# Two sequences' expert passes: full tiles first, the first sequence's remainders joined to the second's tiles

## The chip, the cores and the metric

One core of a Trainium2 chip. The metric is the device time of one execution in microseconds (us). TensorE (PE, with PEld for its weight loads), VectorE (DVE), ScalarE (ACT), GpSimd (POOL) and SyncE (SP, which issues most DMAs) each run their own program and wait for one another through semaphores.

## The reference

Input x is 2 sequences of 2048 tokens of 256 values. The kernel computes two blocks:

```
x = x + layernorm(attention(layernorm(x)))          # one head of 128, rope, full softmax
x = x + layernorm(ffn(layernorm(x)))

ffn(z): twice:
    zn     = rmsnorm(z) * norm_w
    scores = softmax(zn @ router_w)                  # 8 experts
    two best experts of each token, gates normalised to sum 1
    z      = z + sum over the two: gate * (silu(zn @ w1[e]) * (zn @ w3[e])) @ w2[e]   # 256 -> 512 -> 256
```

## The kernel before

**Shape of the program.** The first 385 us hold the attention of both sequences. In the attention of the second, DVE slips in the routing of the first sequence, and splits the expert weights into pairs of fp16 numbers. Then come four expert passes in the order (loop 0, sequence 0), (0, 1), (1, 0), (1, 1), numbered k = 0 to 3, and a tail in which the second sequence's last results are combined, normalised and stored.

**Tiles.** A pass treats one sequence: 2 x 2048 = 4096 rows (a token once for each of its experts), sorted by expert and padded to whole tiles of 128 rows for each expert. With 8 experts that is at most 32 + 7 = 39 tiles (`TILES`), and the pass always runs 39, whatever the data: a tile that holds no rows costs as much as a full one. A tile t goes like this:

- POOL `fetch` (L1620) gathers 128 rows of fp16 pairs (`x_pair`), four tiles ahead; SP `turn` (L1566) turns them with a transposing DMA into `e_xT`, two tiles ahead.
- PE `inner` (L1966): 12 matmuls into `psum_a`, 12 into `psum_b`. ACT takes silu of the first (L1708); DVE `gate` (L1888) multiplies the two.
- At the start of the next tile PE `turn_h` (L1974) turns the product; ACT (L1703) and DVE `h_lo` (L1881) split it into two fp16 halves. PE then does `inner` of the next tile and only after that `outer` (L1985, 12 matmuls) of this one. ACT copies the result out (`y_copy`, L1714), POOL `send` (L1629) scatters it to `expert_rows`.

So every engine's program is a list of tiles, and PE's order is turn_h(t-1), inner(t), helpers, outer(t-1), helpers.

**Helpers beside the tiles.** While pass k runs, the other sequence's next routing (number r = k + 1) is made in the tiles of the pass, in an order written by hand in `expert_pass`: `quad` in tiles 3 to 14 (SP loads results in `load_half`, L1547; DVE `combine` adds them, L1754 and L1760; PE `turn_z`, L1928, and `logits`, L603; ACT squares and copies), then `stage` with one step per tile in tiles 15 to 32: logits, softmax, `pick_best` twice (L440 to L449), gate values (L455 to L462), counts (L471, L477), `expert_starts` (L483 to L488), `expert_rows_of_tiles` (L493 to L495), `rows_of_tokens` (L501 to L511), `experts_of_tiles` (L559 to L562), `mark_tiles` (L516), four times `mark_lanes` of 8 (L523), and indices (L540 to L551). Beside steps 3 to 10 run `row_hi` (ACT, L1680), `row_lo` (DVE, L1815) and `store_rows` (SP, L1555 on), which write the rows that the next pass will gather. On DVE a helper comes after `gate` of its tile and before the `h_lo` that follows:

```python
for u in range(UNROLL):
    ...
        h_lo(s - 1)
    gate(s)
    if join:
        join(u, "end")
```

`link(...)` makes DVE wait for the end of the instruction just issued, so linked instructions run strictly one after another. A small part of the four passes is a hardware loop (`Fori`) over groups of three tiles: on ACT and DVE the quads, on PE only the quads and the `last` groups of k = 3 and one group in each other pass. In the tail SP loads each quarter of the last results, DVE combines it and takes its statistics.

Of the kernel before, what the change touches and what calls it, by code (L numbers as in the profile page):

```python
# [34 lines left out]
TILES = 2 * S // P + NE - 1  # L35
ROWS = TILES * P
# [15 lines left out]
ARENA = 17760  # L52
# [16 lines left out]
def sandwich_kernel(nc, x, wq, wk, wv, wo, norm_w, router_w, w1, w3, w2, rope, out, sorted_rows, expert_rows, token_rows):  # L69
    with ExitStack() as ctx:  # L70
# [58 lines left out]
        sources = sb("token_of_row", [P, B, TILES], U32)  # L129
        targets = sb("result_row_of_row", [P, B, TILES], U32)  # L130
        expert_sb = sb("expert_of", [P, B * TILES], I32)
        gates = gates_sb[:, :].rearrange("p (h k t) -> p h k t", h=B, k=2)
        expert_of = expert_sb[:, :].rearrange("p (h t) -> p h t", h=B)
        rank_sb = sb("rank_down", [P, NE])
        tile_row_sb = sb("tile_row", [P, TILES])
# [17 lines left out]
        def routing_space(large, both, small, row):  # L153

            wide = [large(C) for _ in range(8)]
            return Routing(*wide, both(2 * C), small(4 * NT).rearrange("p (k t) -> p k t", k=4),
                           small(2 * NT).rearrange("p (k t) -> p k t", k=2), small(2 * NT).rearrange("p (k t) -> p k t", k=2),
                           [small(2 * NT).bitcast(I32) for _ in range(3)], small(4 * NE).rearrange("p (k e) -> p k e", k=4),
                           small(NE).bitcast(I32), small(TILES * NE), small(TILES), row(4 * TILES))

        front = take(NT * TILES + NT)
        hot_t = front[:, 0 : NT * TILES].bitcast(F16)
        squares, sum_sq = front[:, 0:D], front[:, NT * TILES : NT * TILES + NT]
        zT = take(2 * 2 * D).rearrange("p (half u c t) -> p half u c t", half=2, u=2, c=DC)
        later_routing = routing_space(take, take, take, lambda n: front[:, D : D + n])
# [40 lines left out]
        first_routing = routing_space(pieces(shared), pieces(xT_words[0][:, D : 2 * D]), pieces(wqkv_words),  # L206
                                      pieces(tab[:, NT * P + NT * TILES :]))
# [131 lines left out]
        x_split = [t.bitcast(F16).rearrange("r d -> (r d)")[0 : S * 2 * D].rearrange("(r d) -> r d", d=2 * D) for t in sorted_rows]  # L339
# [67 lines left out]

        def shifted_logits(dve, link, r):
# [4 lines left out]
            if r:  # L413
                dve.wait_ge(s_rms, r + 1)
                nc.vector.tensor_scalar(factor[:, h, :], root, X_SCALE, None, ALU.mult).then_inc(s_factor, 1)
# [64 lines left out]
        def expert_starts(dve, link, r):  # L480
            R = routing[r > 0]
            total, padded, upper, start = (R.start_f[:, q, :] for q in range(4))
            link(nc.vector.tensor_copy(total, tok_exp(R.sum)[:, NT - 1, :]))  # L483
            link(nc.vector.tensor_scalar(R.start_i, total, float(P - 1), None, ALU.add))
            link(nc.vector.tensor_scalar(R.start_i, R.start_i, -P, None, ALU.bitwise_and))
            link(nc.vector.tensor_copy(padded, R.start_i))
            link(nc.vector.tensor_tensor_scan(upper, padded, zero_tile[:, 0:NE], 0.0, ALU.add, ALU.add))
            link(nc.vector.tensor_tensor(start, upper, padded, ALU.subtract))  # L488

        def expert_rows_of_tiles(dve, link, r):  # L490
            R = routing[r > 0]

            link(nc.vector.tensor_tensor(R.sum, R.sum, R.both[:, C : 2 * C], ALU.subtract))  # L493
            link(nc.vector.tensor_tensor(R.sum, R.sum, R.both[:, 0:C], ALU.add))
            link(nc.vector.tensor_tensor(tok_exp(R.sum), tok_exp(R.sum), per_expert(R.start_f[:, 3, :]), ALU.add))  # L495
# [1543 lines left out]
```

## Time and profile before

| | |
|---|---|
| median of 3 runs | 1161.94 us (1158.58 to 1163.95) |
| the profiled execution | 1165.51 us, its span 1163.8 us |
| mean granted TensorE clock over the span | 0.961 |
| PE busy, DVE busy, ACT busy, POOL busy | 91%, 61%, 49%, 46% |
| expert passes | first matmul at 392.17 us, the last tile's send at 1118.95 us |

A busy share is a mean over stages that have different limits. What sets the time of a stage is read from the chain that ended last and from the spacing of one instruction from tile to tile.

### The profile page before, as it was taken

How to read it: one execution, taken by the hardware profiler on the slowest of the kernel's cores; microseconds unless marked ns; L12 is line 12 of the kernel's file. 1: busy time of each engine (PE TensorE's matmuls, PEld its weight loads, DVE VectorE, ACT ScalarE, POOL GpSimd, SP SyncE). 2: the span in 40 equal slices, each digit the busy share in tenths (PEclk: the TensorE clock that was granted, in tenths of full speed). 3: DMA queues.
4: the chain of work that ended last, by engine and by line, in shares of the span. 5: the costliest groups of instructions: out<-in, count | busy, mean ns of one | idle time of the engine just before them, and what ended most of it. 6: DMA issues, size and time to landing. Idle time of an engine off the chain costs nothing.

```text
span 1163.8 us, 24709 instructions
## 1 busy us (share of the span) xinstructions
PE 1057.8 (91%) x7506; PEld 723.6 (62%) x7507; DVE 705.4 (61%) x1598; ACT 574.5 (49%) x1117; POOL 532.8 (46%) x699
## 2 busy tenths in 40 slices
PE   4799998788999599999999999999999999999930
PEld 3478886556888266666667666666766666656620
DVE  5779988869887244576344476444467436544436
ACT  3566666557987234553345553345464333333312
POOL 2412234956776453444443544444444444544315
PEclk9899999879999799999999999999999999999975
DMA  9900000000000222353365254365355346433344
GB/s 313 338 1 0 0 0 1 1 15 20 17 18 6 55 84 76 96 154 88 92 154 150 79 145 109 91 161 136 88 131 125 88 127 173 107 94 88 82 148 159
DMA packets 146311, 110.81 MB, mean 95 GB/s; under 512 B 92592, under 2 KB 132144, under 8 KB 146224
## 3 DMA queue, kind: packets, MB, share of 16 engines
q1 hardware_dynamic: 131248, 68.72, 22.9%
q0 software_dynamic: 14976, 40.91, 11.8%
q8 instruction: 56, 0.92, 0.3%
q14 instruction: 31, 0.25, 0.1%
HBM read 56.11 MB, written 33.03 MB: 77 GB/s over the span
## 4 chain that ended last, share of the span: by engine, by line
PE 62%; DVE 2%; DMA 1%; issue 1%; ACT 0%; POOL 0%; ACTq 0%; SPq 0%; DVEq 0%; POOLq 0%
PE psum_s L1966 36%; PE psum_o L1985 18%; PE psum_s L1974 6%; PE psum_t L603 2%; PE psum_t L1928 1%; DVE arena L1754 1%; DMA arena<-expert_rows 0%; DVE f_stats L1780 0%; DMA arena<-arena 0%; DMA arena<-sorted_rows,token_of_row 0%; DVE arena L1760 0%; DMA expert_rows<-arena,result_row_of_row 0%; PE psum_t L531 0%; DVE f_tmp L360 0%; DVE arena L1888 0%
## 5 line engine op out<-in xcount | busy, mean ns | idle before, releaser
L1966 PE MATMUL psum_s<-w_all,arena 128*128 x1872 | 432.9, 381 | 12.8 <-DMA arena<-arena 11.2
L1629 POOL DMA_INDIRECT expert_rows<-arena,result_row_of_row x156 | 156.1, 1000 | 359.0 <-ACT arena L1714 356.1
L1966 PEld LDWEIGHTS psum_s<-w_all,arena 128*128 128x128 f16 x1872 | 174.3, 98 | 213.2 <-issue 22.8
L1888 DVE SCALAR_TENSOR_TENSOR arena<-psum_s,gate_scale,arena 128x512 f32<-128x512 f32 x156 | 117.1, 751 | 206.6 <-ACT arena L1708 98.8
L1985 PE MATMUL psum_o<-w_all,arena 128*128 x1872 | 229.9, 273 | 1.5 <-DVE arena L1881 1.5
L1985 PEld LDWEIGHTS psum_o<-w_all,arena 128*128 128x128 f16 x1872 | 181.9, 98 | 47.7 <-issue 3.6
L1881 DVE TENSOR_TENSOR arena<-psum_s,arena 128x512 f16<-128x512 f32 x156 | 107.5, 689 | 147.8 <-ACT arena L1703 114.8
L1714 ACT ACTIVATE arena<-psum_o 128x256 f32<-128x256 f32 x156 | 59.8, 383 | 251.1 <-PE psum_o L1985 247.3
L1620 POOL DMA_INDIRECT arena<-sorted_rows,token_of_row x156 | 153.2, 982 | 52.3 <-issue 46.0
L1708 ACT ACTIVATE arena<-psum_s,silu_scale 128x512 f32<-128x512 f32 x156 | 107.4, 688 | 125.9 <-PE psum_s L1966 73.2
L1703 ACT ACTIVATE arena<-psum_s 128x512 f16<-128x512 f32 x156 | 93.1, 597 | 21.4 <-PE psum_s L1974 14.9
L1340 PE MATMUL psum_s<-arena 128*128 128x512 f16 x384 | 94.4, 398 | 1.4 <-DVE arena L1116 1.4
L1974 PE MATMUL psum_s<-ident,arena 128*128 128x128 f32 x624 | 94.2, 274 | 1.0 <-DVE arena L1888 0.8
L823 ACT ACTIVATE arena<-psum_t 128x512 f32<-128x512 f32 (+1 forms) x128 | 69.7, 595 | 45.6 <-PE psum_t L1335 45.2
L875 ACT ACTIVATE arena<-psum_s,arena,alpha 128x1024 f32<-128x1024 f32 x64 | 76.5, 1199 | 25.4 <-DVE arena L1144 25.3
L1127 DVE TENSOR_REDUCE arena<-psum_s 128x1 f32<-128x1024 f32 x64 | 77.8, 1216 | 12.7 <-PE psum_s L1340 12.6
L1335 PE MATMUL psum_t<-ident,arena 128*128 128x128 f32 x512 | 68.2, 276 | 9.1 <-ACT arena L875 5.8
L1974 PEld LDWEIGHTS psum_s<-ident,arena 128*128 128x128 f32 x624 | 73.3, 142 | 4.1 <-DVE arena L1888 2.4
L1335 PEld LDWEIGHTS psum_t<-ident,arena 128*128 128x128 f32 x512 | 59.3, 143 | 17.9 <-ACT arena L875 7.2
L1340 PEld LDWEIGHTS psum_s<-arena 128*128 (+1 forms) x384 | 39.2, 103 | 44.2 <-issue 7.6
L1380 PE MATMUL psum_o<-arena 128*128 128x128 f32 x512 | 64.1, 278 | 0.0
L1380 PEld LDWEIGHTS psum_o<-arena 128*128 128x128 f32 x512 | 59.7, 192 | 0.0
(238 smaller groups left out, 1223.4 us busy)
## 6 DMA issues: line engine op xcount, KB each, us to landing
w_all<-in_L_ffn_w SPq DMA_DIRECT2D x24, 512.0 KB, 10.1
arena<-expert_rows SPq DMA_DIRECT2D x48, 256.0 KB
sorted_rows<-w_all SPq DMA_DIRECT2D x24, 256.0 KB
arena<-expert_rows SPq DMA_DIRECT2D x8, 512.0 KB, 5.5
out<-x_sb SPq DMA_DIRECT2D x8, 512.0 KB, 6.4
arena<-sorted_rows,token_of_row POOLq DMA_INDIRECT x156
arena<-arena SPq DMA_TRANSPOSE x156
expert_rows<-arena,result_row_of_row POOLq DMA_INDIRECT x156
```

Of the source, the lines that this page charges most:

```text
L1335: last = nc.tensor.transpose(psum_t[g % 2][:, k * P : (k + 1) * P], probs[:, kc * P : (kc + 1) * P], ident[:, :])
L1340: last = nc.tensor.matmul(psum_s[:, kb * 512 : (kb + 1) * 512], qkT[:, lq, 0, bass.ds(i * P, P)], qkT[:, lk, 1, kb * 512 : (kb + 1) * 512] ...
L1380: last = nc.tensor.matmul(psum_o[:, 0:P], v_whole[:, kc, :], pT_whole[:, (kc - HALVED) * P : (kc - HALVED + 1) * P], start=False, stop=(kc ...
L1620: nc.gpsimd.indirect_dma_start(x_pair[:, u, :, :].rearrange("p l d -> p (l d)"), None, x_split[h], bass.IndirectOffsetOnAxis(ap=sources[:, ...
L1629: nc.gpsimd.indirect_dma_start(expert_rows[h][:, :], bass.IndirectOffsetOnAxis(ap=targets[:, h, t : t + 1], axis=0), y_row[:, u, :], None) ...
L1703: nc.scalar.activation(hT[:, 0, :, :].rearrange("p c t -> p (c t)"), psum_h, ACT.Copy).then_inc(s_h_hi, 1)
L1708: nc.scalar.activation(silu_a, psum_a, ACT.Silu, scale=silu_scale[:, 0:1]).then_inc(s_silu, 1)
L1881: nc.vector.tensor_tensor(hT[:, 1, :, :].rearrange("p c t -> p (c t)"), psum_h, hT[:, 0, :, :].rearrange("p c t -> p (c t)"), ALU.subtract ...
L1888: nc.vector.scalar_tensor_tensor(h_row, psum_b, gate_scale[:, 0:1], silu_a, ALU.mult, ALU.mult).then_inc(s_h, 1)
L1966: last = nc.tensor.matmul(bank, e_xT[:, u, lx * DC + c, :], w_split[:, bass.ds(e * EW + at, FF)], start=(q == 0), stop=(q == 3 * DC - 1))
L1974: last = nc.tensor.transpose(psum_h[:, c * P : (c + 1) * P], h_row[:, c * P : (c + 1) * P], ident[:, :])
L1985: last = nc.tensor.matmul(psum_e, hT[:, lh, c, :], w_split[:, bass.ds(e * EW + at, D)], start=(q == 0), stop=(q == 3 * FC - 1))
```

## The change

The first sequence's pass of a loop (k = 0 and 2) now takes only full tiles of its experts, exactly 25 (`FULL`; 32 tiles' worth of rows over 8 experts always hold at least 25 full ones). The rows that are left are carried: they join the rows of the second sequence, in a pass of 46 tiles (`MIXED`, k = 1 and 3). The carried rows come first there, in at most 14 tiles (`CARRY`), whose free rows the second sequence fills. A loop then has 71 tiles and the kernel 142, where it had 156. Both sequences' gathered rows of a loop lie in one DRAM buffer, and all results in `token_rows`. The first sequence's results are complete after tile 13 of the mixed pass, so its combine starts there in tile 18, not in the next pass. The index arithmetic (`expert_starts`, `expert_rows_of_tiles`, `experts_of_tiles`, `row_indices`) gets more steps. All loops of the passes are written out (no `Fori`), and a table of plans says in which tile each helper runs. The first half of the output is stored from within the last pass, and the tail's four loads are issued together.

```diff
+FULL = TILES - 2 * (NE - 1)                       # 25
+CARRY = TILES - FULL                              # 14
+MIXED = 2 * B * S // P + NE - 1 - FULL            # 46
...
-            link(nc.vector.tensor_scalar(R.start_i, total, float(P - 1), None, ALU.add))
-            link(nc.vector.tensor_scalar(R.start_i, R.start_i, -P, None, ALU.bitwise_and))
-            link(nc.vector.tensor_copy(padded, R.start_i))
-            link(nc.vector.tensor_tensor_scan(upper, padded, zero_tile[:, 0:NE], 0.0, ALU.add, ALU.add))
-            link(nc.vector.tensor_tensor(start, upper, padded, ALU.subtract))
+        def full_tiles_first(dve, link, r):        # r = 0 and 2: 15 linked instructions, 2 others (was 6)
+            nc.vector.tensor_copy(total, counted)
+            link(nc.vector.tensor_copy(R.start_i, counted))
+            link(nc.vector.tensor_scalar(R.start_i, R.start_i, -P, None, ALU.bitwise_and))
+            link(nc.vector.tensor_copy(full, R.start_i))
+            link(nc.vector.tensor_tensor_scan(own, full, zero_tile[:, 0:NE], 0.0, ALU.add, ALU.add))
...
+        def rest_tiles_first(dve, link, r):        # r = 1 and 3: 10 linked, 2 others
+            nc.vector.tensor_tensor(own, rest_rows, rest, ALU.subtract)
+            nc.vector.tensor_tensor(shift, rest_start, rest, ALU.add)
+            link(nc.vector.tensor_tensor(total, tok_exp(R.sum)[:, NT - 1, :], rest, ALU.add))
...
+            link(nc.vector.tensor_tensor(beyond, tok_exp(R.sum), own, ALU.is_ge))
+            nc.vector.tensor_tensor(tok_exp(R.both[:, 0:C]), tok_exp(R.sum), shift, ALU.add)
+            link(nc.vector.tensor_tensor(beyond, beyond, step, ALU.mult))
+            link(nc.vector.tensor_tensor(R.sum, R.both[:, 0:C], R.both[:, C : 2 * C], ALU.add))
...
+                for q, threshold in enumerate((carried[:, 2, :], start)):      # r = 1 and 3
+                    link(nc.vector.tensor_tensor(cmp, tile_row.unsqueeze(2).to_broadcast(shape),
+                                                 threshold.unsqueeze(1).to_broadcast(shape), ALU.is_ge))
+                    link(nc.vector.tensor_reduce(R.expert[:, q, :], cmp, AX.X, ALU.add))
...
+        PASS = (FULL, MIXED, FULL, MIXED)
+        Plan = namedtuple("Plan", "load combine root logits softmax pick1 pick2 gates counts starts ranks places experts marks lanes split index")
+        plans = (Plan(None, 3, None, 12, 13, 13, 14, 14, 15, 15, 16, 16, 17, 17, (0,) * 18 + (11, 11, 10), 3, 21),
+                 Plan(16, 18, 26, 27, 28, 29, 30, 31, 32, 33, 34, 35, 36, 36, (0,) * 37 + (8, 8, 8, 8), 27, 41),
+                 Plan(1, 3, 11, 12, 13, 13, 14, 14, 15, 15, 16, 16, 17, 17, (0,) * 18 + (11, 11, 10), 12, 21),
+                 Plan(16, 18, 26, *(None,) * 14))
+        OUT = 29
...
+                    if k and t == plan.load:
+                        for u in range(UNROLL):
+                            sp.wait_ge(s_sent[u], landed(u, FIRST[k] + (CARRY if k % B else 0)))
+                        for p in range(2):
+                            load_half(k, p)
+                    if k and 2 <= t - plan.combine + 1 < PAIRS:
+                        load_half(k, t - plan.combine + 1)
+                    if k < END and 0 <= t - plan.split - 1 < PAIRS:
+                        store_rows(k, t - plan.split - 1)
+                    if k == END and 2 <= t - OUT < 2 + PAIRS and (t - OUT) % 2 == 0:
+                        store_out((t - OUT - 2) // 2)
```

In the plans a number is a tile of the pass. `combine` = c means one pair of token tiles in each of the tiles c to c + 7 on DVE, with `turn_z`, `logits` and ACT's part one tile later; `split` = s means `row_hi`, `row_lo` and `store_rows` in the tiles s + 1 to s + 8; `lanes` gives the number of lane marks in each tile. Before, `combine`, `turn_z` and `logits` took two of every three tiles.

## Rows read from the trace of the kernel before

**Rows 1.** The page: chain that ended last, by line.

```profile
PE psum_s L1966 36%; PE psum_o L1985 18%; PE psum_s L1974 6%; PE psum_t L603 2%; PE psum_t L1928 1%; DVE arena L1754 1%; DMA arena<-expert_rows 0%; DVE f_stats L1780 0%; DMA arena<-arena 0%; DMA arena<-sorted_rows,token_of_row 0%; DVE arena L1760 0%; DMA expert_rows<-arena,result_row_of_row 0%; PE psum_t L531 0%; DVE f_tmp L360 0%; DVE arena L1888 0%
```

**Rows 2.** That chain in order of time: start, us, what; the start, and two plain tiles.

```profile
385.67 3.04 DMA arena<-sorted_rows,token_of_row
388.73 3.32 DMA arena<-arena
392.17 5.23 PE psum_s L1966 x12
...
1106.53 2.62 PE psum_s L1966 x12
...
1110.89 2.64 PE psum_s L1966 x12
```

**Rows 3.** Timeline of POOL: first send of passes 0, 1, 3, and the last.

```profile
403.78 1.01 POOL L1629 DMA_INDIRECT expert_rows<-arena,result_row_of_row  x1 [8.03 <-ACT arena L1714]
...
585.79 0.97 POOL L1629 DMA_INDIRECT expert_rows<-arena,result_row_of_row  x1 [2.11 <-ACT arena L1714]
...
949.96 0.98 POOL L1629 DMA_INDIRECT expert_rows<-arena,result_row_of_row  x1 [2.10 <-ACT arena L1714]
...
1118.95 0.97 POOL L1629 DMA_INDIRECT expert_rows<-arena,result_row_of_row  x1 [2.45 <-ACT arena L1714]
```

**Rows 4.** Timeline of DVE in pass 1: start, us, line, operation, idle before.

```profile
672.97 0.75 DVE L1888 SCALAR_TENSOR_TENSOR arena<-psum_s,gate_scale,arena 128x512 f32<-128x512 f32 x1 [1.47 <-PE psum_s L1966]
673.63 0.28 DVE L440 TENSOR_REDUCE arena<-arena 128x16 f32<-128x128 f32 x1
...
675.62 0.88 DVE L1815 SCALAR_TENSOR_TENSOR w_all<-arena,row_factor,w_all 128x256 f16<-128x256 f32 x2
676.41 0.68 DVE L1881 TENSOR_TENSOR arena<-psum_s,arena 128x512 f16<-128x512 f32 x1
677.32 0.75 DVE L1888 SCALAR_TENSOR_TENSOR arena<-psum_s,gate_scale,arena 128x512 f32<-128x512 f32 x1 [0.22 <-issue]
...
682.46 0.17 DVE L455 TENSOR_TENSOR arena<-arena 128x16 f32<-128x16 f32 x1
...
683.86 0.88 DVE L1815 SCALAR_TENSOR_TENSOR w_all<-arena,row_factor,w_all 128x256 f16<-128x256 f32 x2
...
687.24 0.41 DVE L471 COPY arena<-psum_y 128x256 f32<-128x256 f32 x1
...
688.52 0.88 DVE L1815 SCALAR_TENSOR_TENSOR w_all<-arena,row_factor,w_all 128x256 f16<-128x256 f32 x2
...
691.62 0.16 DVE L483 COPY arena<-arena 128x8 f32<-128x8 f32 x1
...
692.85 0.93 DVE L1815 SCALAR_TENSOR_TENSOR w_all<-arena,row_factor,w_all 128x256 f16<-128x256 f32 x2
...
700.34 0.48 DVE L501 TENSOR_TENSOR arena<-arena 128x128 f32<-128x128 f32 x2
...
702.07 0.88 DVE L1815 SCALAR_TENSOR_TENSOR w_all<-arena,row_factor,w_all 128x256 f16<-128x256 f32 x2
...
709.06 1.45 DVE L516 TENSOR_TENSOR arena<-tile_of_row,tile_numbers 128x1248 f16<-128x1248 f32 x1
...
713.41 1.87 DVE L523 TENSOR_SCALAR arena<-lane_numbers,lane_of_row,token_numbers 128x128 f16<-128x128 f16 x8
```

**Rows 5.** Windows: us, busy of PE, PEld, DVE, ACT, POOL, granted clock, DMA share, GB/s.

```profile
392.00:396.00 4.00, 3.83 (x10) 1.35 (x11) 0.00 (x0) 0.69 (x1) 2.84 (x3) 0.50 0.38 100
...
280.00:290.00 10.00, 7.97 (x68) 5.91 (x66) 9.58 (x24) 7.08 (x13) 6.76 (x12) 1.00 0.04 14
...
950.00:1001.00 51.00, 50.66 (x317) 30.86 (x316) 31.58 (x65) 19.12 (x35) 23.98 (x24) 1.00 0.64 166
1064.00:1112.00 48.00, 47.92 (x306) 29.78 (x305) 20.88 (x38) 17.66 (x33) 17.97 (x19) 1.00 0.30 75
```

**Rows 6.** The page's DMA issues: KB each, median us to landing.

```profile
arena<-expert_rows SPq DMA_DIRECT2D x8, 512.0 KB, 5.5
```

More of the change, by code:

```diff
@@ L151, in sandwich_kernel, with routing_space @@
         C = NT * NE
-        def routing_space(large, both, small, row):
+        def routing_space(large, both, small, row, tiles, cmp):
             wide = [large(C) for _ in range(8)]
@@ L1604, in _ @@
+            for c in range(QUADS, B * QUADS):
+                store_out(c)
             sp.wait_ge(s_out, 16 * B * QUADS)
@@ L1733, in _, with h_hi @@
-            for k in range(len(order)):
-                experts(k)
+                        square(r, 2 * p + g)
+                    copy_zT(act, r, p, p % 2)
+                if t == plan.logits + 1:
+                    exps(act, r)
+                if 0 <= t - plan.split - 1 < PAIRS:
+                    row_hi(k, t - plan.split - 1)
+            def h_hi(s):
+                act.wait_ge(s_th, s + 1)
+                nc.scalar.activation(hT[:, 0, :, :].rearrange("p c t -> p (c t)"), psum_h, ACT.Copy).then_inc(s_h_hi, 1)
@@ new lines, in beside @@
+                        first_z(1, t - plan.combine)
+                if k and t == plan.root:
+                    mean_square(r)
+                if t == plan.split:
+                    row_factor(dve, r)
+                if t == plan.logits:
+                    shifted_logits(dve, link, r)
+                if t == plan.softmax:
+                    softmax(dve, link, r)
+                if t == plan.pick1:
+                    pick_best(dve, link, r, 0)
+                if t == plan.pick2:
+                    pick_best(dve, link, r, 1)
@@ new lines, in beside @@
+                if t == plan.gates:
+                    gate_values(dve, link, r)
+                if t == plan.counts:
+                    counted_tiles(dve, link, r)
+                if t == plan.starts:
+                    expert_starts(dve, link, r)
+                if t == plan.ranks:
+                    expert_rows_of_tiles(dve, link, r)
+                if t == plan.places:
+                    rows_of_tokens(dve, link, r)
+                if t == plan.experts:
+                    experts_of_tiles(dve, link, r)
@@ new lines, in beside @@
+                if t == plan.marks:
+                    dve.wait_ge(s_rows, r + 1)
+                    dve.wait_ge(s_eid, r + 1)
+                    dve.sem_inc(s_held, 1)
+                    mark_tiles(hot_t, slots_of(r))
+                if t < len(plan.lanes):
+                    mark_lanes(hot_p, sum(plan.lanes[0:t]), plan.lanes[t])
+                if t == plan.index:
+                    read_tokens(dve, link, r)
+                    row_indices(dve, link, r)
+                if 0 <= t - plan.split - 1 < PAIRS:
+                    row_lo(k, t - plan.split - 1)
@@ L2013, in _, with beside @@
-            for k in range(len(order)):
-                experts(k)
+            def beside(k, plan, t):
+                r = B + k - 1
+                if 0 <= t - plan.combine - 1 < PAIRS:
+                    turn_z(r, t - plan.combine - 1)
+                if t == plan.counts:
+                    counts(pe, r)
+                for part in range(PARTS):
+                    if t == min(plan.index - PARTS + 1 + part + (k % B == 0), plan.index):
+                        tokens_of_rows(pe, r, hot_t, hot_p, token_sums[1], part)
```

688 lines of the change are left out of this document (319 added, 369 removed).

## The prediction, made before the changed kernel ran

> **What bounds the kernel now.** I read the page's chain first. Two thirds of it is PE in the expert passes [rows 1], next to nothing else: for 727 us the end moves only with the matmuls. The chain in order of time then gives the cost of one tile without helpers: `inner` starts at 1106.53 and, one tile on, at 1110.89, so 4.36 us, of which 2.62 are `inner` itself [rows 2]. The timeline of POOL gives the passes: from the first send of pass 0 to that of pass 1 are 182.0 us [rows 3], of which 39 x 4.36 = 170.0 are tiles and 12.0 the PE helpers (`turn_z`, `logits`, counts, tokens) and small waits. Pass 3 has no PE helpers; its 38 intervals take 169.0 [rows 3] against 165.7, so 3.3 are lost.
>
> The timeline of DVE shows how near it comes to mattering. A helper starts 0.66 after its `gate`, and the next `h_lo` follows it. With 2.78 us of helpers (673.63 to 676.41) the next `gate` came at 677.32, 4.35 after the last, and waited only 0.22 [rows 4]. So a tile has room for about 2.78 us of helpers; what is beyond delays `h_lo`, behind which PE's `outer` and DVE's own next `gate` are queued, and so every following tile by the excess.
>
> **What is removed.** 156 - 142 = 14 tiles. Helpers stay, once for each routing, so what goes are tiles at the plain price: 14 x 4.36 = 61.0 us. ACT's, DVE's, POOL's and SP's share of these tiles goes too, and all lies behind PE. Bounds: nothing in the pass runs faster than the plain tile, and the mean tile costs 182.0/39 = 4.67, which would be 65.3; I take 61.0, since the helper work is not removed.
>
> **Loops written out.** Pass 3 is the one in which most of PE's groups loop. I take it that its 3.3 us are the price of the looping and come back, and about 0.2 from the other passes' single looped group: 3.5. Bounds: 0, if they are small waits of another kind that stay, and 4.
>
> **DVE helpers, packed closer.** Passes 0 and 2 have 25 tiles where 39 held the same routing, so steps share tiles. Costs from [rows 4]: `pick_best` 1.99 (673.63 to 675.62, 6 linked steps, 0.33 each), so softmax (3 steps) about 0.95; gate values 1.40; counts 1.28; six small linked steps 1.23, so 0.205 each; `rows_of_tokens` 1.73; a compare or reduce goes by its elements, 0.28 for 128 and 1.45 for 1248 (`mark_tiles`), so 0.53 for 368; eight lanes 1.87 to the end of the last, 0.22 apart; `row_lo` 0.80 (675.62 to 676.41).
>
> Pass 0, excess over 2.78:
> tile 13, softmax and first pick 2.94: 0.16. Tile 14, second pick and gates 3.39: 0.61. Tile 15, counts 1.28 and `rest_tiles_first` (10 linked, 2 others) 2.25: 0.75. Tile 16, ranks (5 linked steps of 0.33 and one of 0.2) 1.86 and places 1.73: 0.81. Tile 17, four compares and reduces over 368 elements at 0.57, two small steps 0.4, marks over 46 tiles for 39 (1.71), 4.39: 1.61. Tiles 18 to 21 (lanes 2.45, indices, six linked small steps and five others, about 2) fit. Sum 3.9.
>
> Pass 2 has `row_lo` in tiles 13 to 20 as well, 0.80 more in each: 0.96, 1.41, 1.55, 1.61, 2.41, then 0.47 twice (11 lanes, 3.25) and 0.24: 9.1.
>
> Pass 1 has room: only tile 33, `full_tiles_first` (15 linked, 2 others, 3.28) with `row_lo`, 4.08, exceeds: 1.3.
>
> Together 14.3 us. Bounds: nothing, if PE helpers in the same tiles or ACT's slack give DVE more room than the row shows; and 20, if each such tile also loses some 0.4 to ACT or SP lateness.
>
> **DVE in the second attention.** Routing 0 has 9 more linked steps and one or two others (2.0), two more linked steps and one other for the ranks (0.86), and a compare and a reduce over 200 elements in place of 312 (0.23 less): 2.6. Where it runs DVE is busy 9.58 of 10 us and PE only 7.97 [rows 5], so DVE sets the pace there and I take all 2.6; the bounds are 0, if PE's work there covers it, and 2.6.
>
> **What is moved and costs nothing.** First-sequence combine now sits in tiles 18 to 25 of the mixed passes, in every tile and not in two of three. It is four instructions of the size of `row_lo`'s two, so 4 x 0.40 = 1.6 on DVE (2.4 in pass 3 with two statistics), under 2.78. PE's `turn_z` and `logits` are the same count. The first fetch of a pass waits on POOL for the indices: made in tile 21 of 25, fetch and turn took 3.04 and 3.32 at the start [rows 2], and the rows are needed three tiles (13 us) on; the `send` queued behind the waiting fetch has as long, since `y_row` has three buffers. If that cover goes, each of three pass starts costs up to these 6.4 us. The tail keeps its DVE chain; its first-half stores were off the chain already.
>
> **Sum.** On the profiled execution's 1165.5: minus 61.0, minus 3.5, plus 14.3, plus 2.6 = 1117.9. That execution lies 3.6 above the median of 1161.9, so 1114.3: 1114 us.
>
> **Rivals.**
> *DVE's room is larger.* No stall beyond noise, and attention hides its part: 1114.3 - 14.3 - 2.6 = 1097; with a few remaining, 1099. For it: DVE is busy only 61% of the span. Against: the one row at 2.78 had no more than 0.22 left.
>
> *Loads come late.* A load of results is now issued one tile before its combine, it was two. In pass 3: the load waits for the pair two before (gate + 2.3) and is wanted at the gate two tiles on + 0.66, 9.4, leaving 7.1 us. A load of 512 KB, in pairs of 1 MB, landed in 5.5 [rows 6], and ours are pairs of 256 KB. But DMA share in the loading stretch of pass 3 was 0.64 for 51 us and 0.30 in plain tiles [rows 5]: eight loads took 17.3, 2.2 each, so a tile with its own load wants 1.3 + 2.2 of 4.36, 0.80. If queueing makes each late by 1 to 2 us in one mixed pass (8 tiles), DVE waits in `combine`, `h_lo` behind it: plus 8 to 16, 1122 to 1130.
> The Trainium skill (DMA: Bandwidth & Descriptors, the fixed and variable cost) would give, as an estimate, 2.0 us and 0.5 MB at 436 GB/s, 3.2 us, for such a pair alone, well in time, and the sum would stay as it is; no row here shows one alone.
>
> *Slower than before: the clock falls.* PE now meets idle gaps in passes 0 and 2 up to 2.4 us in a row of tiles. The first `inner` of pass 0, after PE had waited for fetch and turn, took 5.23, twice its 2.62 [rows 2], at a granted clock of 0.50, the 1.2 GHz level [rows 5]. At that level a tile costs 4.4 more, so from 13 such tiles on the 47.6 us of the forecast and another 5.8 are gone, and the time is 1168 or more. Against: from 280 to 290 PE idled 2 of 10 us and the clock stayed at 1.00 [rows 5].
> The skill (TensorE: Matmul & The Clock Gate, Part 1) has the clock fall when the engine idles; the first tile's 0.50 agrees.
>
> **How the numbers follow.** Forecast (14 tiles gone, DVE stalls of about this size) 0.60, own range 1106 to 1121. Room larger, near 1099: 0.16. Loads or a pass start late, near 1125: 0.19. Clock 0.02. Something that eats the gain entirely, near no change: 0.03 with chances split. The range 1100 to 1128 leaves out the lower half of the second case, some of the third, and the last two. A measurement here can tell about 0.5%, 5.8 us; the first three cases are all faster by more: faster 0.95, same 0.02, slower 0.03.
>
> **What would show it.** Sends 4.36 apart in plain tiles, 142 of them; in pass 2 gates 5 to 7 us apart in tiles 14 to 18, with PE waiting for L1881's successor there; pass 3 without the spread of intervals up to 4.8; no wait of `combine` for a DMA. I am wrong if combine waits show in passes 1 or 3, if DVE's stalls are absent, or if PE idles at a pass start.

## The result and the profile after

The changed kernel took 1109.52 us as a median of four runs (1107.38 to 1113.16), the kernel before 1160.26 (1158.06 to 1163.95) on the same chip: a ratio of 0.9563 with a 95% interval of 0.9523 to 0.9603. The forecast was 1114 in a range of 1100 to 1128. The profiled execution of after took 1107.38 us (span 1105.6), that of before 1165.51 (span 1163.8).

The page of after: busy times, the granted clock in 40 slices, the chain by engine and by line, and the issues of the loads of results.

```profile
PE 993.7 (90%) x7114; PEld 685.1 (62%) x7114; DVE 699.1 (63%) x1628; ACT 552.1 (50%) x1075; POOL 508.5 (46%) x671
...
PEclk9999999969899889999999999999999999999985
...
PE 56%; DVE 6%; issue 1%; DMA 1%; ACT 0%; POOL 0%; ACTq 0%; DVEq 0%; SPq 0%; POOLq 0%
PE psum_s L2002 32%; PE psum_o L2021 16%; PE psum_s L2010 5%; PE psum_t L675 2%; PE psum_t L1970 1%; DVE arena L1805 1%; DVE arena L1927 1%; DVE arena L1934 1%; DMA arena<-token_rows 0%; DVE f_stats L1819 0%; DVE w_all L1849 0%; DMA arena<-arena 0%; DMA arena<-sorted_rows,token_of_row 0%; ACT L697 0%; DMA token_rows<-arena,result_row_of_row 0%
...
arena<-token_rows SPq DMA_DIRECT2D x48, 256.0 KB, 3.2
```

PE still carries the chain (L2002, L2021 and L2010 are `inner`, `outer` and `turn_h`), but `h_lo` (L1927) and `gate` (L1934) of DVE are in it with a per cent each and `row_lo` (L1849) with less than half of one, where [rows 1] had next to nothing of them: DVE now holds PE in places. From 395.5 to 1058 us, the passes, the granted clock was 1.00.

Who waited for what from 370 us to the end (us in total, times, longest):

```profile
DVE arena L1805 <- DMA arena<-token_rows: 10.3, 1, 10.3
PE psum_o L2021 <- DVE arena L1927: 10.0, 11, 1.8
```

PE's `outer` waited for `h_lo` 11 times, never over 1.8 us. `combine` (L1805) waited for a DMA once, in the tail after the last tile; in the passes it never did.

The time is best read from the `gate` of each pass' first tile. The timeline of DVE, after: the first `gate` of passes 0 to 3, and that of the last tile.

```profile
395.69 0.75 DVE L1934 SCALAR_TENSOR_TENSOR arena<-psum_s,gate_scale,arena 128x512 f32<-128x512 f32 x1 [14.76 <-PE psum_s L2002]
519.33 0.75 DVE L1934 SCALAR_TENSOR_TENSOR arena<-psum_s,gate_scale,arena 128x512 f32<-128x512 f32 x1 [1.44 <-PE psum_s L2002]
733.99 0.75 DVE L1934 SCALAR_TENSOR_TENSOR arena<-psum_s,gate_scale,arena 128x512 f32<-128x512 f32 x1 [1.41 <-PE psum_s L2002]
861.55 0.75 DVE L1934 SCALAR_TENSOR_TENSOR arena<-psum_s,gate_scale,arena 128x512 f32<-128x512 f32 x1 [1.40 <-PE psum_s L2002]
1058.02 0.75 DVE L1934 SCALAR_TENSOR_TENSOR arena<-psum_s,gate_scale,arena 128x512 f32<-128x512 f32 x1 [1.29 <-PE psum_s L2002]
```

The same gates of before started at 397.43, 579.46, 761.60, 943.63 and 1113.57. "Over" is the length less the 4.36 us of a plain tile for each tile (pass 3: each interval between its tiles).

| stretch | before, us (tiles, over) | after, us (tiles, over) | change of the over | forecast |
|---|---|---|---|---|
| pass 0 | 182.03 (39, 12.0) | 123.64 (25, 14.6) | +2.6 | +3.9 |
| pass 1 | 182.14 (39, 12.1) | 214.66 (46, 14.1) | +2.0 | +1.3 |
| pass 2 | 182.03 (39, 12.0) | 127.56 (25, 18.6) | +6.6 | +9.1 |
| pass 3, first to last gate | 169.94 (38, 4.3) | 196.47 (45, 0.3) | -4.0 | -3.5 |
| first to last gate | 716.14 | 662.33 | -53.8 = -61.0 + 11.2 - 4.0 | -50.2 |

The spans differ by 58.2: 53.8 here, 1.7 before the first gate and 2.7 after the last.

The crowded tiles are where they were forecast. Tile 16 of pass 2 in the timeline of DVE, after: ranks and places (L536 to L557), then `row_lo`, between one `gate` and the next.

```profile
817.44 0.73 DVE L1934 SCALAR_TENSOR_TENSOR arena<-psum_s,gate_scale,arena 128x512 f32<-128x512 f32 x1
818.10 0.27 DVE L536 TENSOR_TENSOR arena<-arena 128x128 f32<-128x128 f32 x1
...
821.65 0.88 DVE L1849 SCALAR_TENSOR_TENSOR w_all<-arena,row_factor,w_all 128x256 f16<-128x256 f32 x2
822.44 0.68 DVE L1927 TENSOR_TENSOR arena<-psum_s,arena 128x512 f16<-128x512 f32 x1
823.04 0.74 DVE L1934 SCALAR_TENSOR_TENSOR arena<-psum_s,gate_scale,arena 128x512 f32<-128x512 f32 x1
```

Neither `h_lo` nor `gate` waited for anything: DVE is busy without a gap. The helpers took 4.34 us (818.10 to 822.44), and the interval is 5.60 = 4.34 + 0.66 before them + 0.60 after them. So where DVE never waits 4.36 - 1.26 = 3.10 us of helpers fit. It is the same in the one over-full tile of pass 1: 4.18 us of helpers (675.22 to 679.40) and an interval of 5.45. The 2.78 of [rows 4] was the length that happened to be there and not the limit; that row itself has 0.91 us from `h_lo` to the next `gate`, where 0.60 is enough here. The intervals into tiles 14 to 18 of pass 2 were 5.43, 5.27, 5.65, 5.60 and 6.51 (the last after `experts_of_tiles` and `mark_tiles`), those of pass 3 all 4.35 to 4.43, but one of 4.52.

Windows of after: the crowded tiles of pass 2, and pass 3 (us, busy of PE, PEld, DVE, ACT, POOL, granted clock, DMA share, GB/s).

```profile
799.00:850.00 51.00, 45.60 (x315) 28.05 (x314) 44.64 (x144) 25.10 (x49) 21.26 (x20) 1.00 0.46 117
861.00:1050.00 189.00, 188.99 (x1216) 118.44 (x1215) 91.31 (x176) 71.70 (x129) 87.45 (x86) 1.00 0.50 123
```

In pass 3 PE was busy 188.99 of 189 us. In the crowded 51 us it was idle 5.4 us in pieces, and the clock stayed at 1.00.

### The profile page after: what moved, and what is told of

Same layout as the page of the kernel before. It is cut to its first block, busy times and chain, and to the rows that moved or that the text cites. A ratio compares the mean times of both kernels' runs of the same rounds, so it can differ in the third digit from the quotient of the medians.

```text
span 1105.6 us, 22718 instructions
## 1 busy us (share of the span) xinstructions
PE 993.7 (90%) x7114; PEld 685.1 (62%) x7114; DVE 699.1 (63%) x1628; ACT 552.1 (50%) x1075; POOL 508.5 (46%) x671
## 3 DMA queue, kind: packets, MB, share of 16 engines
q0 software_dynamic: 13632, 37.24, 11.3%
## 4 chain that ended last, share of the span: by engine, by line
PE 56%; DVE 6%; issue 1%; DMA 1%; ACT 0%; POOL 0%; ACTq 0%; DVEq 0%; SPq 0%; POOLq 0%
PE psum_s L2002 32%; PE psum_o L2021 16%; PE psum_s L2010 5%; PE psum_t L675 2%; PE psum_t L1970 1%; DVE arena L1805 1%; DVE arena L1927 1%; DVE arena L1934 1%; DMA arena<-token_rows 0%; DVE f_stats L1819 0%; DVE w_all L1849 0%; DMA arena<-arena 0%; DMA arena<-sorted_rows,token_of_row 0%; ACT L697 0%; DMA token_rows<-arena,result_row_of_row 0%
## 5 line engine op out<-in xcount | busy, mean ns | idle before, releaser
L2002 PE MATMUL psum_s<-w_all,arena 128*128 x1704 | 393.8, 381 | 12.0 <-DMA arena<-arena 11.2
L1688 POOL DMA_INDIRECT token_rows<-arena,result_row_of_row x142 | 144.5, 1018 | 319.6 <-ACT arena L1770 316.8
L2002 PEld LDWEIGHTS psum_s<-w_all,arena 128*128 128x128 f16 x1704 | 158.5, 98 | 193.5 <-issue 19.4
L2021 PE MATMUL psum_o<-w_all,arena 128*128 x1704 | 209.4, 273 | 10.0 <-DVE arena L1927 10.0
L1934 DVE SCALAR_TENSOR_TENSOR arena<-psum_s,gate_scale,arena 128x512 f32<-128x512 f32 x142 | 106.5, 750 | 171.4 <-PE psum_s L2002 170.1
L2021 PEld LDWEIGHTS psum_o<-w_all,arena 128*128 128x128 f16 x1704 | 164.7, 98 | 54.1 <-issue 15.4
L1927 DVE TENSOR_TENSOR arena<-psum_s,arena 128x512 f16<-128x512 f32 x142 | 97.9, 689 | 132.1 <-ACT arena L1758 131.7
L1674 POOL DMA_INDIRECT arena<-sorted_rows,token_of_row x142 | 142.2, 1002 | 60.0 <-issue 42.9
L1763 ACT ACTIVATE arena<-psum_s,silu_scale 128x512 f32<-128x512 f32 x142 | 97.6, 687 | 111.1 <-PE psum_s L2002 111.1
L2010 PE MATMUL psum_s<-ident,arena 128*128 128x128 f32 x568 | 86.1, 274 | 0.8 <-DVE arena L1934 0.8
L2010 PEld LDWEIGHTS psum_s<-ident,arena 128*128 128x128 f32 x568 | 67.3, 144 | 2.7 <-DVE arena L1934 1.3
L1805 DVE SCALAR_TENSOR_TENSOR arena<-arena,gates 128x256 f32<-128x256 f32 x128 | 54.3, 489 | 10.3 <-DMA arena<-token_rows 10.3
```

The lines of the kernel that those rows point to most:

```text
L1674: nc.gpsimd.indirect_dma_start(x_pair[:, u, :, :].rearrange("p l d -> p (l d)"), None, rows, bass.IndirectOffsetOnAxis(ap=sources[:, at : ...
L1688: nc.gpsimd.indirect_dma_start(rows, bass.IndirectOffsetOnAxis(ap=targets[:, at : at + 1], axis=0), y_row[:, u, :], None).then_inc(s_sent[ ...
L1763: nc.scalar.activation(silu_a, psum_a, ACT.Silu, scale=silu_scale[:, 0:1]).then_inc(s_silu, 1)
L1927: nc.vector.tensor_tensor(hT[:, 1, :, :].rearrange("p c t -> p (c t)"), psum_h, hT[:, 0, :, :].rearrange("p c t -> p (c t)"), ALU.subtract ...
L1934: nc.vector.scalar_tensor_tensor(h_row, psum_b, gate_scale[:, 0:1], silu_a, ALU.mult, ALU.mult).then_inc(s_h, 1)
L2002: last = nc.tensor.matmul(bank, e_xT[:, u, lx * DC + c, :], w_split[:, bass.ds(e * EW + at, FF)], start=(q == 0), stop=(q == 3 * DC - 1))
```

## The experiments

**1. Before, with the loops written out.** Only PE's list of tiles in the kernel before changes: its `Fori` loops over groups of tiles become plain ones.

```diff
-            if looped or k == END:
+            if looped:
...
-                with eng.Fori(1 + QUADS + staged, GROUPS - 1) as i:
-                    group(i, None, False, False)
+                for i in range(1 + QUADS + staged, GROUPS - 1):
+                    group(i, None, False, False)
```

> The kernel before, with PE's list of tiles written out in all passes (DVE and ACT keep their loops). If the 4.3 us that pass 3 lost over plain tiles (first to last gate 169.9 us for 38 intervals of 4.36) are the price of PE's loop, pass 3 falls to 165.7 to 166.2 us and its intervals of 4.46 to 4.62 become 4.36; passes 0 to 2 stay at 182.0 to 182.2 within 0.4. If they come from DVE (combine with statistics, 2.4 us of helpers) or from loads of results, nothing changes in pass 3.

One execution: 1155.04 us, before on that chip 1159.20. The timeline of DVE, this kernel: first and last `gate` of pass 3.

```profile
937.06 0.75 DVE L1896 SCALAR_TENSOR_TENSOR arena<-psum_s,gate_scale,arena 128x512 f32<-128x512 f32 x1 [1.39 <-PE psum_s L1974]
...
1102.94 0.75 DVE L1896 SCALAR_TENSOR_TENSOR arena<-psum_s,gate_scale,arena 128x512 f32<-128x512 f32 x1 [1.29 <-PE psum_s L1974]
```

Pass 3 took 165.88 from gate to gate, where before took 169.94: 4.06 us came back, all that the changed kernel gained there (4.0), and passes 0 to 2 hardly moved (181.99, 181.58 and 181.91, 0.7 less together). DVE and ACT kept their loops, so it is PE's looping that cost this. The loops are their own term.

**2. Pass 0 with its row splits in the tiles of pass 2.**

```diff
-        plans = (Plan(None, 3, ..., (0,) * 18 + (11, 11, 10), 3, 21),
+        plans = (Plan(None, 3, ..., (0,) * 18 + (11, 11, 10), 12, 21),
```

> The changed kernel, with the row splitting of pass 0 in tiles 13 to 20 as in pass 2, not in 4 to 11. If the stalls are DVE's helpers beyond a tile's room, pass 0 (123.6 us) gets 4 us longer and shows pass 2's intervals (5.4, 5.3, 5.7, 5.6, 6.5 into tiles 14 to 18). If pass 2 is slower for its loads and squares, which pass 0 does not have, pass 0 stays within 1 us of 123.6.

One execution: 1115.79 us. Pass 0 took 127.55, 3.9 more than in the changed kernel, and its intervals into tiles 14 to 18 are 5.32, 5.28, 5.61, 5.61 and 6.50, those of pass 2. So `row_lo` beside a step is the whole difference of the two passes: it is free where the tile has room and costs its length where it has none.

**3. DVE's room, measured.** In tiles 1 to 12 of pass 3, which have no such helper, tile t got t + 6 lane marks with no use, linked once for each tile.

```diff
+                if 1 <= t <= 12:
+                    for q in range(t + 6):
+                        ins = nc.vector.tensor_scalar(hot_p[:, q * P : (q + 1) * P], lane_of[:, :], place_lane[:, 0:1],
+                                                      token_no[:, 0:1], ALU.is_equal, ALU.mult)
+                    link(ins)
```

> The changed kernel, with 7, 8, ... 18 more lane marks (0.22 us apart) on DVE behind the gate of the tiles 1 to 12 of pass 3, which have no helpers. This is extra work whose results nobody reads. If a tile has 2.8 us of room and all beyond it delays PE one for one, the intervals stay at 4.36 up to 12 marks (tile 6) and then grow by 0.22 each, to about 5.6 behind tile 12, 4.1 us in all. If the room is 3.3 us, they grow only from 15 marks on, to 5.1, 1.4 us in all.

One execution: 1115.86 us. The timeline of DVE, this kernel: tiles with 15, 17 and 18 marks (L1916).

```profile
905.37 0.75 DVE L1939 SCALAR_TENSOR_TENSOR arena<-psum_s,gate_scale,arena 128x512 f32<-128x512 f32 x1
906.04 3.45 DVE L1916 TENSOR_SCALAR arena<-lane_numbers,lane_of_row,token_numbers 128x128 f16<-128x128 f16 x15
909.53 0.69 DVE L1932 TENSOR_TENSOR arena<-psum_s,arena 128x512 f16<-128x512 f32 x1
910.29 0.75 DVE L1939 SCALAR_TENSOR_TENSOR arena<-psum_s,gate_scale,arena 128x512 f32<-128x512 f32 x1
...
915.44 0.74 DVE L1939 SCALAR_TENSOR_TENSOR arena<-psum_s,gate_scale,arena 128x512 f32<-128x512 f32 x1
916.10 4.07 DVE L1916 TENSOR_SCALAR arena<-lane_numbers,lane_of_row,token_numbers 128x128 f16<-128x128 f16 x17
920.21 0.69 DVE L1932 TENSOR_TENSOR arena<-psum_s,arena 128x512 f16<-128x512 f32 x1
920.82 0.74 DVE L1939 SCALAR_TENSOR_TENSOR arena<-psum_s,gate_scale,arena 128x512 f32<-128x512 f32 x1
921.47 4.29 DVE L1916 TENSOR_SCALAR arena<-lane_numbers,lane_of_row,token_numbers 128x128 f16<-128x128 f16 x18
925.80 0.69 DVE L1932 TENSOR_TENSOR arena<-psum_s,arena 128x512 f16<-128x512 f32 x1
926.41 0.74 DVE L1939 SCALAR_TENSOR_TENSOR arena<-psum_s,gate_scale,arena 128x512 f32<-128x512 f32 x1
```

With 15 marks the helpers took 3.49 us (906.04 to 909.53) and the interval 4.92: 3.49 - 0.56 = 2.93 were free. With 17 and 18 they took 4.11 and 4.33, the intervals 5.38 and 5.59: 3.09 and 3.10 free. With 12 marks (2.85 us) the interval was still 4.37, and with 13 (3.06) it was 4.53, so the first tile of this ramp had 2.89 free. The tile after the run paid 0.41 once. All together 4.4 us, which is what a limit of 2.95 in each of the six tiles from 13 marks on would cost. The forecast's 2.78 is thus 0.1 too small where the work grows slowly and 0.3 too small in full tiles; a room of 3.3 is out.

**4. One tile more in the mixed passes.**

```diff
-MIXED = 2 * B * S // P + NE - 1 - FULL
+MIXED = 2 * B * S // P + NE - 1 - FULL + 1
```

> The changed kernel, with 47 tiles in the mixed passes, one each that holds no rows. If a tile without helpers costs its 4.36 us on PE whether it holds rows or not, first gate to last gate becomes 662.3 + 8.7 = 671.0 us (0.2 more for wider marks). If an empty tile were cheaper, for its gathers and scatters of one row, it would be under 668.

One execution: 1122.12 us. First to last gate is 671.17, 8.84 over the changed kernel's 662.33 for two tiles that hold no rows: 4.4 each. This is the price at which the 14 tiles went.

**5. Gate values and tile experts later.** In passes 0 and 2 both move into tiles with room (14 to 22, 17 to 23); the wait of `mark_tiles` on the experts is left out there, since it doesn't read them.

```diff
-Plan(..., 14, 14, 15, 15, 16, 16, 17, 17, ...)
+Plan(..., 14, 22, 15, 15, 16, 16, 23, 17, ...)
...
-                    dve.wait_ge(s_eid, r + 1)
+                    if k % B:
+                        dve.wait_ge(s_eid, r + 1)
```

> The changed kernel, with the gate values of passes 0 and 2 made in tile 22 and the experts of the next pass's tiles in tile 23, where there were no helpers; they stood in the crowded tiles 14 and 17. If stalls are DVE's work beyond a tile's room, the interval into tile 15 falls to about 4.5 and that into tile 18 to about 4.4, so pass 0 loses some 1.8 us and pass 2 some 2.8: 4.6 us less between first and last gate (662.3 before this edit), about 0.4% of the whole. If work only moves its cost, because tiles 22 to 24 have no room either or the next pass waits for the experts, the 662.3 stays.

1104.15 us as a median of 4 (1103.56 to 1109.14), ratio to before 0.9514 (0.9489 to 0.9538). First to last gate fell from 662.33 to 658.97: pass 0 by 1.5 and pass 2 by 1.8, 3.4 of the 4.6 hoped for. The interval into tile 18 fell from 5.72 to 4.73 and from 6.51 to 5.03, but the intervals into tiles 20 and 21 of pass 2 rose from 4.71 and 4.58 to 5.06 and 4.80. Lane marks with `row_lo` hold 3.25 and 3.02 us there, and by DVE alone these intervals would be 4.51 and 4.36: `gate` waited 0.48 and 0.43 us for PE as well. What made PE late there stays open.

**6. The second attention with routing 0 spread out.** One step of routing 0 for each attention step, gate values and experts at the end.

```diff
             pick_best(dve, link, 0, 1)
-            gate_values(dve, link, 0)
...
-            expert_starts(dve, link, 0)
-            expert_rows_of_tiles(dve, link, 0)
             split_lo(odd(3))
             step(NT + 4, True, True, True, True, False, 1)
+            expert_starts(dve, link, 0)
+            split_lo(odd(4))
+            step(NT + 5, True, True, True, True, False, 2)
+            expert_rows_of_tiles(dve, link, 0)
             rows_of_tokens(dve, link, 0)
-            experts_of_tiles(dve, link, 0)
...
+            experts_of_tiles(dve, link, 0)
+            gate_values(dve, link, 0)
```

> The changed kernel, with routing 0 spread over more steps of the second attention: the index chain one step after the counts, ranks and places one step later still, tile marks before the sum over them, gate values and experts near the attention's end. The same instructions, in other steps. In the changed kernel the four steps from the counts on took 14.28, 9.65, 7.60 and 7.85 us, where a step without routing takes 7.84, and before the change 9.46, 10.35, 7.46 and 7.85. If a step has slack on DVE of some 0.7 us and the long step idles PE for nearly 5 us, spreading gives back 4 to 5 us of the attention and the passes stay at 662.3. If DVE is the bound over the whole stage, the same work takes the same time, within 1 us.

1106.13 us as a median of 4 (1104.83 to 1107.17), ratio 0.9519 (0.9503 to 0.9536). Four attention steps from the counts on took 34.4 us, in the changed kernel 39.4; a later step rose from 7.8 to 8.5 where `mark_tiles` went. Between one DVE instruction (L1194) at 243.85 and at 372.07 the changed kernel took 128.22 us for the stage, this one 122.92 (246.79 to 369.71): 5.3 less in all. First to last gate is 662.42, unchanged. The two timelines are read in the last section.

**7. Both, and pass 2's row splits moved away from the routing.**

```diff
+        ROW_TILES = (range(4, 12), range(28, 36), (12, 12, 14, 17, 18, 19, 20, 21))
-                 Plan(1, ..., 14, 14, 15, 15, 16, 16, 17, 17, (0,) * 18 + (11, 11, 10), 12, 21),
+                 Plan(1, ..., 14, 23, 15, 15, 16, 16, 24, 17, (0,) * 18 + (8, 8, 8, 8), 12, 22),
```

> Both edits together, and in pass 2 the row splits in the tiles 12, 12, 14, 17, 18, 19, 20 and 21, eight lane marks in each of the tiles 18 to 21, and the indices in tile 22. By DVE's room, pass 2 keeps only the excess of tiles 13, 15 and 16, some 1.5 us in all, so it falls from 127.6 to about 122 and first to last gate from 662.3 to about 655; with the attention's 4 to 5 the whole is 11 to 12 us faster than the changed kernel, near 1098, 5.4% under the kernel before. If the later indices make pass 3 wait for its first rows (fetch and turn need 6.4 us of the 13 that are left), some of it comes back as PE waiting for the turn at the start of pass 3.

1104.53 us as a median of 5 (1099.66 to 1105.91), ratio 0.9491 (0.9470 to 0.9512). Pass 2's crowded intervals fell by 4.5 us together (4.80, 4.77, 4.82, 5.00, 4.58), but the interval into the first tile of pass 3 was 8.46 us, and first to last gate 660.70. The timeline of PE and a window, this kernel, at the change of pass:

```profile
855.12 0.91 PE L2015 MATMUL psum_s<-ident,arena 128*128 128x128 f32 x4 [2.21 <-DVE expert_of L636]
855.87 4.19 PE L2007 MATMUL psum_s<-w_all,arena 128*128 x12
...
861.65 2.76 PE L2007 MATMUL psum_s<-w_all,arena 128*128 x12
```

```profile
855.00:860.00 5.00, 4.88 (x17) 2.14 (x18) 0.76 (x2) 1.28 (x2) 1.56 (x2) 0.66 0.42 105
```

PE waited 2.21 us for `expert_of` (L636), from which it reads the expert of pass 3's first tile and which now came in the last tile of pass 2; and after that wait the granted clock was 0.66 on average, so that `inner` took 4.19 and not 2.76. My expectation had named late indices as the danger; the row names the expert numbers, and the timeline of DVE bears it out: L636 ended at 855.07, and PE went on at 855.12.

**8. Indices, gates and experts one tile earlier again.**

```diff
-        ROW_TILES = (..., (12, 12, 14, 17, 18, 19, 20, 21))
+        ROW_TILES = (..., (12, 12, 12, 14, 17, 18, 19, 20))
-... 14, 23, 15, 15, 16, 16, 24, 17, (0,) * 18 + (8, 8, 8, 8), 12, 22),
+... 14, 22, 15, 15, 16, 16, 23, 17, (0,) * 17 + (2, 10, 10, 10), 12, 21),
```

> The changed kernel with the attention order of the spread run, the gates and expert numbers in tiles 22 and 23 in passes 0 and 2, and pass 2's eight row splits in tiles 12, 12, 12, 14, 17, 18, 19 and 20 with 2, 10, 10 and 10 lane marks in tiles 17 to 20, so that the indices stay in tile 21 as in the changed kernel. Theory (what a crowded tile costs is VectorE's work beyond some 3.1 us, and the wait at the start of pass 3 in the run with the indices in tile 22 came from those indices alone): pass 0 is 122.2 us as there; pass 2 is 122 to 123 us and the interval into the first tiles of pass 3 is 4.5 us, not 8.46; first gate to last gate some 655 to 656 us. With the spread attention's 4.3 us the whole is some 10 to 11 us under the changed kernel: 1098 to 1101 us as a median. Rival A (that wait has another cause, the row splits that end late or the stores behind them): the interval at the start of pass 3 stays near 8 us although the indices are back in tile 21, first to last gate 659 us or more. Rival B (three row splits in one tile hold up ScalarE or the transposes): pass 2's interval into tile 13 is over 6 us, and the sum stays at 657 to 659 us.

1103.96 us as a median of 6 (1099.92 to 1104.98), ratio 0.9498 (0.9474 to 0.9522). The interval into the first tile of pass 3 is 4.46 again, as it should be if the expert numbers were the cause. This run moved the indices, the experts and the last row split a tile earlier together, so it does not part them; that it was the experts rests on the row of run 7. But the intervals into tiles 13 and 14 of pass 2 are 7.35 and 6.45, and first to last gate is 660.38. The timeline of ACT, then that of PE, and a window, this kernel:

```profile
794.51 1.70 ACT L1741 ACTIVATE w_all<-arena,row_factor 128x256 f16<-128x256 f32 x4 [1.58 <-DVE row_factor L417]
798.55 0.91 ACT L1741 ACTIVATE w_all<-arena,row_factor 128x256 f16<-128x256 f32 x2 [2.34 <-DMA sorted_rows<-w_all]
```

```profile
801.12 1.67 PE L2026 MATMUL psum_o<-w_all,arena 128*128 x12 [3.26 <-DVE arena L1932]
802.57 1.06 PE L2015 MATMUL psum_s<-ident,arena 128*128 128x128 f32 x4
803.43 3.88 PE L2007 MATMUL psum_s<-w_all,arena 128*128 x12
```

```profile
800.00:805.00 5.00, 3.88 (x20) 2.70 (x21) 3.92 (x11) 4.08 (x7) 3.20 (x3) 0.73 0.71 159
```

Two row splits ran at once; the third waited 2.34 us for the store of the first, since there is room for two in `row_split`. ACT waited there, DVE's `row_lo` behind it, `h_lo` behind that, PE 3.26 us behind that, and once more the granted clock was low afterwards: 0.73 in the 5 us from 800 on, and `inner` took 3.88.

**9. Two row splits in a tile at most.**

```diff
-        ROW_TILES = (..., (12, 12, 12, 14, 17, 18, 19, 20))
+        ROW_TILES = (..., (12, 12, 14, 17, 17, 18, 19, 20))
-... (0,) * 17 + (2, 10, 10, 10), 12, 21),
+... (0,) * 18 + (11, 11, 10), 12, 21),
```

> The run before it with pass 2's row splits in tiles 12, 12, 14, 17, 17, 18, 19 and 20 (two in a tile at most) and the lane marks 11, 11 and 10 in tiles 18 to 20; all else as there. Theory (in the run before, the third row split of tile 12 waited for the store of the first one, 2.3 us, because two rows have a place in memory, and the two intervals after it paid 3.0 and 2.1 us): those 5.1 us go, the intervals into tiles 13 and 14 of pass 2 are 4.4 and 4.9 us, tiles 17 to 20 carry 3.4 to 3.5 us of VectorE's work each against some 3.1 of room and pay 1.5 to 2.5 us more than before; pass 2 is 123 to 124.5 us, the interval into the first tiles of pass 3 stays at 4.46 us, first gate to last 656.5 to 658 us, and the median 2.5 to 4 us under the run before, 1100 to 1101.5 us. Rival (the intervals of 7.35 and 6.45 us come from the row splits' work alone and not from a store): two in tile 12 still cost a part, into tile 13 over 5.5 us, and the sum stays at 659 us or more.

1099.95 us as a median of 5 (1096.74 to 1101.72), ratio to before 0.9450 (0.9432 to 0.9469). The intervals into tiles 13 and 14 of pass 2 are 4.35 and 4.79, pass 2 is 123.14, pass 3 begins with 4.46, and first to last gate is 656.67. Pass 2, the start of pass 3 and the sum fell where the theory had them. One of its terms did not: the four intervals behind the tiles 17 to 20 (4.76, 4.56, 5.07, 4.79) are 0.6 us longer together than in run 8, where 1.5 to 2.5 were expected. This is the fastest of the kernels run.

## Why the prediction was right, and where its terms were off

The sum was made on the profiled execution: 1117.9, where that of after took 1107.4. The 10.5 us between them, term by term:

- **14 tiles at 4.36 us.** Right, and run 4 shows an added tile at the same price. The mean tile of 4.67 would have been wrong, since helpers stayed.
- **Loops written out, -3.5.** Measured -4.0 in pass 3, and -4.06 in run 1 by themselves.
- **DVE's stalls, +14.3.** Right in mechanism and place, too large in size: 11.2 (2.6, 2.0 and 6.6 where 3.9, 1.3 and 9.1 were put). The mis-sized term is the room: 3.10 us of helpers are free in a full tile and not 2.78 (pass 2 above, and run 3). The work itself was costed well: the helpers of tiles 13 to 17 of pass 2, with their waits, took 22.2 us; the prediction's costs for them add up to 21.8. With 3.10 for 2.78 its own list gives 2.5, 1.0 and 6.6, together 10.1; and the tile behind each run pays some 0.4 once, which it had not (0.41 in run 3, and 4.77 behind the 5.45 in pass 1), an estimate of 11.3. By passes this misses by 0.3 to 0.6, which no run takes apart. 3.1 us less than forecast.
- **The second attention, +2.6.** Measured +4.3: the three steps after the counts took 27.3 us before and 31.5 after. It is no accident of one execution: from the first to the last L1194 (L1122 before) the stage took 124.0 us or 0.1 less in before and in run 1, and 128.2 to 128.4 in after and in runs 2 to 5. I had costed the added instructions alone (2.9 us by their number, 2.8 by the timeline) and taken the length of each from pass 1. Three of them ran longer here, as the last section shows, by 2.0 us together; the kernel before had one such instruction in this stage, 0.5 longer, that is short now, and 0.2 lie in the step after. The granted clock fell to 0.50 from 276 to 280 us, behind PE's wait of 4.75, but DVE, without a gap there, set the pace.
- **What was put at nothing.** Loads of results issued one tile ahead were in time: no `combine` waited for one in a pass. The Trainium skill (DMA: Bandwidth & Descriptors, the fixed and variable cost) had given, as an estimate, 3.2 us for such a pair, and the profile's page has 3.2. The starts of passes were in time. The tail was not at nothing: from DVE's last addition to the end of the span it is 8.7 us before and 6.3 after. Run 1, which is the old order with loops written out, has 8.6, and runs 2 to 9 have 6.3 to 6.6, so this belongs to the change and not to the execution. It is not the last store: that took 2.9 us to land in both, and its bytes were through 3.6 us after that addition in both. What differs comes behind it: 5.1 us before and 2.8 after in which the profile has neither an instruction nor a packet. The changed kernel has only 4 of the 8 stores of the output in the tail and no hardware loops in the passes, and run 1 rules out PE's loops; beyond that the cause stays open. With 0.3 ahead of it that is -2.7, and the prediction, which had only the DVE chain and the stores in the tail, put nothing for it.
- **Not in the sum.** The first attention of after, whose program is the same, was 5.4 us ahead at its third step: 1.2 from its start and 4.2 by the clock (last section). Run 1, with the program of before, was there as early as after. Some 0.6 lie in small differences.

Together -3.1 - 0.5 + 1.7 - 2.7 - 5.4 - 0.6 = -10.6. Of these the 5.4 belong to the one execution and not to the kernels: without them the forecast of the median, 1114.3, comes down to 1109.1, and 1109.5 was measured. That this comes within 0.4 us is partly luck: the 1114.3 stand on a median of before of 1161.9, and with the 1160.26 of the four runs the same terms give 1107.4, 2.1 under the measured 1109.5. And the forecast itself was helped by terms that cancel: the stalls and the tail on one side, 5.8 us, and the second attention on the other, 1.7.

**The rivals.** *Room larger*, 1099: out as put (run 3 puts the limit at 2.9 to 3.1 us, and stalls show in 11 waits), though the truth lay a fifth of the way to it. *Loads late*: no such wait. *The clock falls in the passes*: it stayed at 1.00 with waits of up to 1.8 us. Runs 7 and 8 show that this had some ground: with single waits of 2.2 and 3.3 us it was 0.66 in the 5 us from 855 on and 0.73 in those from 800 on. The forecast's gaps "up to 2.4 us" were near that, and the real ones smaller.

## What to carry to other kernels

When padded tiles or rounds are cut, take the plain tile as the price and list what each remaining tile must now carry on the second-busiest engine; what fits is the interval less the fixed time before and after the helpers, and a row that fits does not show the limit. When steps are spread over tiles, find out what the last of them feeds: a step put into the last free tile (run 7: 660.70 us from first to last gate) and a third user of two buffers (run 8: 660.38) each left the passes longer than they had been without it (658.97 in run 5). In a stretch in which another engine sets the pace, take the length of an instruction from that stretch and not from a quiet one.

## What the runs showed of the hardware

**DVE's small instructions stretch beside POOL's wide ones.** Second attention, after; the timeline of DVE, then that of POOL, then that of PE.

```profile
270.62 0.58 DVE L507 COPY arena<-arena 128x8 f32<-128x8 f32 x1
...
271.31 0.89 DVE L509 SCALAR_TENSOR_TENSOR arena<-arena 128x8 f32<-128x8 f32 x1
...
272.57 1.12 DVE L537 TENSOR_TENSOR arena<-arena 128x128 f32<-128x128 f32 x1
```

```profile
270.44 0.74 POOL L809 TENSOR_TENSOR x_sb<-x_sb,arena 128x256 f32<-128x256 f32 x1 [2.33 <-ACT arena L932]
271.15 1.04 POOL L784 TENSOR_TENSOR arena<-w_all,scale_g 128x512 f32<-128x512 f32 x1
272.26 1.28 POOL L788 TENSOR_TENSOR w_all<-arena,w_all 128x512 f16<-128x512 f32 x1
```

```profile
276.39 1.97 PE L1407 MATMUL psum_t<-ident,arena 128*128 128x128 f32 x8 [4.75 <-DVE arena L1194]
```

Each of the three ends within 0.15 us of the POOL instruction beside it (271.18, 272.19 and 273.54). In the run that spread the routing the same three lines fall where POOL has nothing of 128x256 or wider under way. The timeline of DVE, run 6:

```profile
279.62 0.17 DVE L507 COPY arena<-arena 128x8 f32<-128x8 f32 x1
...
279.89 0.17 DVE L509 SCALAR_TENSOR_TENSOR arena<-arena 128x8 f32<-128x8 f32 x1
...
286.08 0.29 DVE L537 TENSOR_TENSOR arena<-arena 128x128 f32<-128x128 f32 x1
```

0.58, 0.89 and 1.12 us against 0.17, 0.17 and 0.29: 1.96 us, in a stretch in which PE sat idle 4.75 us for DVE. The Trainium skill (SBUF — State Buffer, Who interferes with whom) has the port pair of DVE and GpSimd as a lock that one holds for its whole instruction; the ends that coincide agree.

**The clock of the first attention differs between executions of one program.** The timeline of PE, before, and then after, at the same instructions:

```profile
50.28 5.30 PE L1340 MATMUL psum_s<-arena 128*128 128x512 f16 x12 [1.42 <-DVE arena L1116]
```

```profile
49.09 2.76 PE L1412 MATMUL psum_s<-arena 128*128 128x512 f16 x12 [1.42 <-DVE arena L1188]
```

The wait ahead of it was 1.42 us in both. The start was 1.2 us apart already at the first matmuls of the kernel, and it still was at this row; the rest came behind it. From 47 to 65 us the granted clock was 0.72 in the profile of before and 1.00 in that of after; in the nine profiles of the experiments, whose programs are alike there, it was 1.00, 0.91, 0.81, 0.72, 1.00, 0.91, 0.72, 0.91 and 0.81, and the third attention step (DVE L1216) came between 66.9 and 73.6 us. Of these 6.7 us, 2.5 were there at the first step's matmuls and 4.2 came behind them: from there to the third step's matmuls it is 14.11 us at a clock of 1.00 (run 5) and 18.33 at 0.72 (run 7). The lower level is 1.2 GHz, at which these 12 matmuls take 5.30 and not 2.76 us. The Trainium skill (TensorE: Matmul & The Clock Gate, Part 1) has the clock fall when the engine idles; the trace agrees that it may, and shows in addition that the same short waits do it in one execution and not in the next. A single execution of this kernel can be up to 4.2 us longer by this, 0.4%, and 2.5 by its start; gate-to-gate times in the passes don't carry either.
